# W_dec in one transfer, the gathers in four steps, the last chunks split singly, and a new order of five engines

## What is computed

```python
# block 1: a linear layer whose matrix is decoded per sequence, then a mixture of 8 experts, 2 per token
U = (mu @ W_dec + b_dec).reshape(B, 129, 30)          # mu: 128 x 64, W_dec: 64 x 3870
param = einsum('bik,kj->bij', U, V)                   # weight = first 128 rows, bias = last row
c = einsum('bsd,bde->bse', x, weight) + bias
gate = c @ Wg.T + bg; scores, idx = top_k(gate, 2); w = softmax(scores)
h = gelu(einsum('td,ehd->teh', c, W1) + b1)           # 8 experts, 256 hidden
x = x + sum over the two chosen of w * (h @ W2 + b2)
# block 2: conditioning, then a gated feed-forward with 512 hidden
h = LN(LN(x; tables by pathway); tables by compartment); t, s: LN(x; tables); m, n, r: x + small MLPs
cat = [w0*h, w1*t, w2*m, w3*n, w4*r, w5*s]            # w = softmax(aw)
y = LN(silu(cat @ int_W1 + int_b1) @ int_W2 + int_b2)
f = silu(y@w1.T*s1) * (y@w2.T*s2); f = gelu(f@h1.T*g1); f = gelu(f@h2.T*g2)
x = x + f @ w3.T * s3
```

## Time and profile before

| | |
|---|---|
| median of three runs | 443.49 us (441.01 to 443.49) |
| profiled execution | 443.04 us, span 441.2 us |
| PE, busy share of the span | 94% |
| DVE | 72% |
| ACT | 66% |
| POOL | 32% |
| mean granted TensorE clock | 0.978 |

### The profile page before, as it was taken

How to read it: one execution, slowest core, us unless ns; L and a number is a source line. 1 busy time by engine, 2 the same in 40 slices (tenths; PEclk the granted TensorE clock), 3 DMA queues, 4 the chain that set the end, 5 groups by cost and what they waited for, 6 DMA issues and landing times.

```text
span 441.2 us, 5719 instructions
## 1 busy us (share of the span) xinstructions
PE 416.0 (94%) x1804; PEld 272.6 (62%) x1804; DVE 315.6 (72%) x651; ACT 290.7 (66%) x515; POOL 142.8 (32%) x129
## 2 busy tenths in 40 slices
PE   4888998999999999999999999999999997999994
PEld 2856544554656765677567665776577646687773
DVE  2889998887985776766886577596784687656542
ACT  1568775797937766497647763975678455776563
POOL 3016896663631650273028261317211012010000
PEclk9799996999999999999999999999999998999999
DMA  8975564473352352532315245035501100000000
GB/s 242 364 293 161 179 174 119 112 229 68 104 155 51 71 163 97 118 99 73 111 40 159 75 116 150 0 70 181 134 3 49 46 3 0 1 0 25 0 25 27
DMA packets 29961, 45.08 MB, mean 102 GB/s; under 512 B 3461, under 2 KB 22378, under 8 KB 29418
## 3 DMA queue, kind: packets, MB, share of 16 engines
q1 hardware_dynamic: 25440, 32.33, 25.7%
q0 software_dynamic: 3584, 10.49, 7.1%
...
## 4 chain that ended last, share of the span: by engine, by line
PE 79%; DVE 8%; ACT 5%; issue 3%; DMA 2%; POOL 2%; another core or an unknown queue 1%; ACTq 0%; POOLq 0%; DVEq 0%
PE bank L644 23%; PE bank L746 20%; PE bank L692 7%; PE bank L636 6%; PE bank L782 6%; PE bank L731 5%; PE bank L823 2%; PE bank L660 2%; DMA muT<-cond_512T_in 2%; PE bank L699 2%; PE bank L771 2%; POOL rstd L1446 1%; ACT mG L890 1%; ACT YN L895 1%
## 5 line engine op out<-in xcount | busy, mean ns | idle before, releaser
L644 PE MATMUL bank<-mG,W 128*128 128x512 f32 x256 | 121.3, 604 | 0.1
L890 ACT ACTIVATE mG<-bank,keepP 128x512 f32<-128x512 f32 x128 | 85.3, 685 | 32.2 <-PE bank L636 30.2
L1446 POOL TENSOR_TENSOR rstd<-ve,mhalf 128x4 f32<-128x4 f32 x24 | 34.0, 1419 | 173.0 <-DVE ve L1196 172.1
L1181 DVE TENSOR_TENSOR mG<-mG,gwbs 128x1024 f32<-128x1024 f32 x64 | 77.1, 1220 | 8.8 <-ACT mG L890 4.4
L644 PEld LDWEIGHTS bank<-mG,W 128*128 128x128 f32 x256 | 48.4, 194 | 44.2 <-issue 39.9
L636 PE MATMUL bank<-ts,A 96*128 96x512 f32 x128 | 66.8, 553 | 1.3 <-ACT mG L890 1.1
L955 ACT ACTIVATE G<-bank,keepP 128x512 f32<-128x512 f32 x48 | 32.8, 696 | 25.4 <-PE bank L746 20.1
L1427 POOL DMA_INDIRECT gp<-pgb_in,ixall x32 | 36.8, 1149 | 27.4 <-DVE norms L1233 17.7
L1430 POOL DMA_INDIRECT gcm<-ctm,ixcm x32 | 36.5, 1140 | 9.8 <-issue 9.8
L746 PE MATMUL bank<-hA_h,h1w_h 128*128 128x512 f32 x96 | 38.9, 405 | 0.0
L746 PE MATMUL bank<-hA_l,h1w_h 128*128 128x512 f32 x96 | 38.6, 402 | 0.0
...
## 6 DMA issues: line engine op xcount, KB each, us to landing
...
```

Source lines behind the costliest of these rows:

```text
L644: mm = pe.matmul(OACC[:, :], W2[:, e * HC + c, :], mG[n % NMG][:, c, :], start=False, stop=(e == E - 1 and c == HC - 1))
L890: act.activation(mG[e % NMG][:, c % HC, :], HM[n % 2][:, :], ACT.Gelu, bias=b1c[:, c:c + 1]).then_inc(m_gelu, 1)
L1181: dve.tensor_tensor(mine, mine, gate.unsqueeze(1).broadcast_to([P, HC, TT, P]), ALU.mult).then_inc(m_q, 1)
L1446: step(pool.tensor_tensor(rstd[:, n, :], ve[:, n, :], mhalf[:, :], ALU.pow))
```

## The change

1. `Wd` comes by one transfer of 128 partitions on SP's queue, with the first half of the columns on the partitions 0 to 63. The last 30 columns go to a place of their own, `wd_u`. The two zero blocks of `Wp` change sides.
2. ACT's queue begins with `muT` (twice), `wd_u` and b_dec; V, `keepP`, `earlyP` and `bdec_u` follow in their old order.
3. The eighth piece of the turning moves from DVE to ACT.
4. The copies of `keepP` that DVE made between the turning and `Uall` (`sq_`, `hs1`, `cs12`) stand behind `Uall`, ahead of the words.
5. `tab` issues two of a tile's 8 indirect DMAs; there are four words `tab0` to `tab3` for a tile.
6. In the tail of tile 7 the last two chunks of layer 2's output are made singly: two high parts and two low parts of 512 columns in place of one of 1024 each.
7. The words of all five engines stand in a new order. (A `tcl` for DVE is defined, and no word calls it.)

```diff
-        Wd = sb("Wd", [P, KR * (DH + 1)], stack=early)
+        Wd = sb("Wd", [P, KR * DH], stack=early)
...
+        wd_u = gap[0:MU, KA + KR:KA + 2 * KR]
...
-        PIECES = ("v", "v", "v", "a", "v", "a", "v", "v")
+        PIECES = ("v", "v", "v", "a", "v", "a", "v", "a")
...
+        def alone(j, k):
+
+            return j is TAIL["p"] and k >= 3 * FC - 2
+
         def tail_lo(eng, j, k):
 
-            eng.wait_ge(p_lo[j.s], j.n * (FC + 4) + (k + 1 if k < FC else FC + (k - FC) // 2 + 1))
+            eng.wait_ge(p_lo[j.s], k + 1 if k < FC else FC + (k - FC) // 2 + 1 + (alone(j, k) and k % 2))
...
             "POOL": (
-                (0, "tcl0 tcl1 tcl2 srt ix tcl3 tab tcl4 tcl5 rt0 tcl6 tcl7 rt1"),
...
+                (0, "ix tcl0 tab0 tab1 tcl1 tcl2 srt tcl3 tab2 tcl4 tab3 tcl5 rt0 tcl6 tcl7 rt1"),
...
-            load(Wd[0:MU, :], A["W_dec"][:, KR * DH:KR * (D + 1)], ld_wd)
+            load(Wd[:, :], A["W_dec"][:, 0:KR * D].rearrange("m (h c) -> h m c", h=2), ld_wd)
...
-                act.wait_ge(p_g[j.s], j.n * 2 * FC + k - FC + 2)
+                w = 1 if alone(j, k) else 2
+                act.wait_ge(p_g[j.s], k - FC + w)
                 dst = hB if k < 2 * FC else hC
-                act.activation(dst[0][:, c:c + 2, j.cols], j.G[:, c:c + 2, j.cols], ACT.Copy).then_inc(p_hi[j.s], 1)
+                act.activation(dst[0][:, c:c + w, j.cols], j.G[:, c:c + w, j.cols], ACT.Copy).then_inc(p_hi[j.s], 1)
...
-            load(Wd[MU:P, 0:KR * DH], A["W_dec"][:, 0:KR * DH], ld_wd)
             for at in (0, MU):
                 load(muT[at:at + MU, :], A["cond_512T"], ld_wd)
+            load(wd_u, A["W_dec"][:, KR * D:KR * (D + 1)], ld_wd)
+            load(bdec, A["b_dec"][:, 0:KR * D].rearrange("o (i k) -> (o i) k", k=KR), ld_bd)
             load(Vk[:, :], A["V"], ld_v)
             load(keepP[:, :], A["keepP"], ld_v)
-            load(bdec, A["b_dec"][:, 0:KR * D].rearrange("o (i k) -> (o i) k", k=KR), ld_bd)
             load(earlyP[:, :], A["earlyP"], ld_small)
...
-            def tables(b):
+            def tables(b, t):
...
-                for t in range(TT):
-                    j = b * TT + t
...
+                j = b * TT + t
```

More of the change, by code:

```diff
@@ L119, in build @@
         DH = D // 2
-        Wd = sb("Wd", [P, KR * (DH + 1)], stack=early)
+        Wd = sb("Wd", [P, KR * DH], stack=early)
         W1T = sb("W1T", [P, E * H], stack=early)
-        gap = sb("gap", [P, 6656 - KR * (DH + 1) - E * H], stack=early)
+        gap = sb("gap", [P, 6656 - KR * DH - E * H], stack=early)
         VT3 = gap[:, 0:KA]
         bdec = gap[:, KA:KA + KR]
-        bdec_u = gap[0:KR, KA + KR:KA + KR + 1]
+        wd_u = gap[0:MU, KA + KR:KA + 2 * KR]
+        bdec_u = gap[0:KR, KA + 2 * KR:KA + 2 * KR + 1]
         earlyP = sb("earlyP", [P, 10 * P + 3 * NI + E + 3], stack=early)
@@ L164, in build @@
         Wp = hs[:, 0:KR * D].rearrange("m (k i) -> m k i", k=KR)
-        wd = [Wd[0:MU, :].rearrange("m (i k) -> m k i", k=KR), Wd[MU:P, 0:KR * DH].rearrange("m (i k) -> m k i", k=KR)]
-        wd_u = Wd[0:MU, KR * DH:KR * (DH + 1)]
-        turned_wd = [Wp[0:MU, :, DH:D], Wp[MU:P, :, 0:DH]]
+        halves = (slice(0, MU), slice(0, DH)), (slice(MU, P), slice(DH, D))
+        wd = [Wd[rows, :].rearrange("m (i k) -> m k i", k=KR) for rows, _ in halves]
+        turned_wd = [Wp[rows, :, cols] for rows, cols in halves]
         warmA = sb("warmA", [2, P], stack=early)
@@ L300, in weights_done @@
         def weights_done(eng, *ns):
-            eng.wait_ge(w_lo, max((3, 1, 2, 4)[n] for n in ns))
+            eng.wait_ge(w_lo, max((3, 2, 4, 1)[n] for n in ns))
         def wide(v, n):
@@ L308, in build @@
             "PE": (
[17 rows of a table removed]
[16 rows of a table added]
             ),
             "ACT": (
[19 rows of a table removed]
[20 rows of a table added]
             ),
             "DVE": (
[15 rows of a table removed]
[16 rows of a table added]
             ),
             "POOL": (
-                (0, "tcl0 tcl1 tcl2 srt ix tcl3 tab tcl4 tcl5 rt0 tcl6 tcl7 rt1"),
-                (1, "tab rt0 -rt2 rt1"),
-                (2, "tab rt0 -rt2 rt1"),
-                (3, "tab -rt2 rt0"),
-                (4, "tab -rt1 rt0 -rt2"),
-                (5, "tab -rt1"),
-                (6, "tab =rt2 -rt0 -rt1"),
-                (7, "tab -rt0 -rt1 =rt2 -rt2 rt0 rt1 rt2"),
[8 rows of a table added]
             ),
             "SP": (
[5 rows of a table removed]
-                (5, "gb0 ^stored -li gb1 -lx gb2 +lr gb3 +lt"),
-                (6, "gb0 ^stored -li gb1 -lx gb2 gb3 +lt li ~stored"),
-                (7, "gb0 -lx gb1 lr gb2 li gb3 ~stored lx =stored -sor sop"),
[8 rows of a table added]
             ),
@@ L1075, in _ @@
             act.wait_ge(ld_wd, 64)
-            act.wait_ge(wp_zero, 1)
+            act.wait_ge(wp_zero, 2)
             for q in range(8):
@@ L1079, in _ @@
                     mine = slice(4 * q, min(4 * q + 4, KR))
-                    act.activation(turned_wd[1][:, mine, :], wd[1][:, mine, :], ACT.Copy)
-                    act.activation(turned_wd[0][:, mine, :], wd[0][:, mine, 0:DH], ACT.Copy).then_inc(wd_act, 1)
+                    act.activation(turned_wd[0][:, mine, :], wd[0][:, mine, :], ACT.Copy)
+                    act.activation(turned_wd[1][:, mine, :], wd[1][:, mine, :], ACT.Copy).then_inc(wd_act, 1)
             load(w12s[:, :], A["w12T"], ld_w[0])
@@ L1098, in wl @@
                 src, dst = staged[n], split[n]
-                dve.wait_ge(w_hi, (2, 1, 3, 4)[n])
+                dve.wait_ge(w_hi, (3, 2, 4, 1)[n])
                 dve.tensor_tensor(flat(dst[1]), src, flat(dst[0]).bitcast(F32), ALU.subtract).then_inc(w_lo, 1)
@@ L1288, in fl_tail @@
                 else:
-                    dst, w = (hB if k < 2 * FC else hC), 2
-                    dve.wait_ge(p_hi[j.s], j.n * (FC + 4) + FC + (k - FC) // 2 + 1)
+                    dst, w = (hB if k < 2 * FC else hC), 1 if alone(j, k) else 2
+                    dve.wait_ge(p_hi[j.s], FC + (k - FC) // 2 + 1 + (alone(j, k) and k % 2))
                 dve.tensor_tensor(dst[1][:, c:c + w, j.cols], j.G[:, c:c + w, j.cols], dst[0][:, c:c + w, j.cols].bitcast(F32),
@@ L1358, in s_m, with tcl @@
                 dve.tensor_scalar(awx[:, 1:2], awx[:, 0:1], -1.0, None, ALU.mult).then_inc(aw_max, 1)
+            def tcl(b):
+                dve.wait_ge(tc_hi, b + 1)
+                dve.wait_ge(ts_stored[b % 2], 16 * ((b - 1) // 2))
+                dve.wait_ge(tc_lo, b)
+                dve.tensor_tensor(tsS[b % 2][32:64, :], tT[b % 2][:, :], tsS[b % 2][0:32, :].bitcast(F32), ALU.subtract).then_inc(tc_lo, 1)
             steps = {"q": q_, "x": x1_, "st": st, "t": t_, "s": s_, "hg": hg, "hc": hc, "oh": oh, "a": a, "flo": flo,
@@ L1363, in _ @@
                      "for": partial(fo_tail, TAIL["r"]), "fop": partial(fo_tail, TAIL["p"]), "al": lambda i, n: al(n), "am": lambda i: s_m(),
-                     "wl": lambda i, n: wl(n), "lm": lambda i: low_sum(), "la": lambda i: low_any(),
+                     "wl": lambda i, n: wl(n), "lm": lambda i: low_sum(), "tcl": lambda i, b: tcl(b), "la": lambda i: low_any(),
                      "tb": lambda i, b: tb(b), "gxl": lambda i, g: gxl(g), "bl": lambda i: b2l(), "gl": lambda i: g96l(), "top": lambda i, g: top(g), "gww": lambda i, g: gww(g),
@@ L1378, in _ @@
             dve.wait_ge(ld_wd, 64)
-            dve.wait_ge(wp_zero, 1)
+            dve.wait_ge(wp_zero, 2)
             for q in range(8):
@@ L1382, in _ @@
                     mine = slice(4 * q, min(4 * q + 4, KR))
-                    dve.tensor_copy(turned_wd[1][:, mine, :], wd[1][:, mine, :])
-                    dve.tensor_copy(turned_wd[0][:, mine, :], wd[0][:, mine, 0:DH]).then_inc(wd_dve, 1)
-            sq_()
-            step(dve.tensor_scalar(hs1[:, :], fsc[:, 0:FC], 0.5, None, ALU.mult))
-            dve.tensor_tensor(cs12[:, :], hs1[:, :], fsc[:, FC:2 * FC], ALU.mult)
+                    dve.tensor_copy(turned_wd[0][:, mine, :], wd[0][:, mine, :])
+                    dve.tensor_copy(turned_wd[1][:, mine, :], wd[1][:, mine, :]).then_inc(wd_dve, 1)
             for q in range(0, 8, 2):
@@ L1403, in _ @@
             ins.then_inc(g8_ready, 1)
+            sq_()
+            step(dve.tensor_scalar(hs1[:, :], fsc[:, 0:FC], 0.5, None, ALU.mult))
+            dve.tensor_tensor(cs12[:, :], hs1[:, :], fsc[:, FC:2 * FC], ALU.mult)
             run(steps, ORDER["DVE"])
@@ L1424, in tables @@
                     weights_done(pool, 3)
-                for t in range(TT):
-                    j = b * TT + t
-                    pool.indirect_dma_start(out=gp[b % 2][:, t, :], out_offset=None, in_=A["pgb"],
-                                            in_offset=bass.IndirectOffsetOnAxis(ap=ixall[:, 0, j:j + 1].bitcast(U32), axis=0))\
-                        .then_inc(gat[b % 2], 16)
-                    pool.indirect_dma_start(out=gcm[b % 2][:, t, :], out_offset=None, in_=CT,
```

(14 more changed lines are left out.)

## The result

The changed kernel takes 468.13 us (median of 4 runs, 466.69 to 469.13), the kernel before 443.49 us beside it. The ratio is 1.0565, with a 95% interval of 1.0516 to 1.0614: it is slower by 5.6%, where the prediction said 434.0 us. The profiled execution took 466.69 us, with a span of 464.7 us and a mean clock of 0.955.

What follows compares the result with a forecast made beforehand. PE was taken as full from 120 to 360 us, so gains lie where it idles or is slowly clocked: 443.04 - 4.5 (start) - 3.5 (tiles 0 and 1) - 1.1 (end) = 434.0 us, range 429.5 to 441.0.

Steps and rivals of the forecast that it cites:

- I take 7.0: Beginning: all of Wd lands at 7.0 us, between 6.3 at the earliest and 7.5, so copying starts 4.1 us sooner.
- Start: Beginning up to tm0: first product at 8.0 us, tm0 at about 17.6; 4.5 us saved, from 1.1 to 5.3.
- Rival B: Beginning: bdec_u still lands at 16.6 us, so the start gives only 1.1 us; 437.3 us in all, chance 0.14.
- Tiles 0 and 1: 46 to 120 us: a slow GpSimd subtraction no longer stops PE at the gate scores; 3.5 us saved, upper bound 5.8.
- rival A: Before 115 us: the saving in tiles 0 and 1 goes to other waits of PE; 437.4 us, chance 0.20.
- 2.0 us: Tiles 0 and 1: DVE's own idle time, the sure part of the saving there.
- Rival D: Tile 0: POOL's root late behind a slow tcl5, so the kernel is slower; 447.0 us, 450.4 with late start; chance 0.07.
- Middle: 120 to 360 us: gathers and roots stay ahead of their readers, PE busy 239 us or more of 240; nothing gained or lost.
- the rest: Everything behind the beginning: 3.5 us saved in tiles 0 and 1, 1.1 at the end, all else at nothing.
- End: Tail of tile 7: single last chunks save 1.1 us (0.6 to 1.4); PE's last wait 1.4 us or less, from 2.21.
- the 1.9 us: Beginning: cost of the first four microseconds of products at clock 0.53, expected to vanish with idle time of about 1.3 us.

Runs made afterwards that it cites:

- b_start: Kernel before with the changed beginning, Wd in two 64-partition transfers, single last chunks, wd_u on its own semaphore, bdec_u ahead of V: 437.91 us, ratio 0.9900.
- b_two: Changed kernel with the old words, gathers and paired last chunks put back, and Wd in two transfers of 64 partitions on SP's queue: 441.41 us, ratio 0.9968.
- a_two: Changed kernel with Wd loaded by two transfers of 64 partitions on SP's queue in place of one of 128: 447.97 us, ratio 1.0108.
- b_gm: Kernel of b_start with only PE's gate scores gm4 and gm5 of tile 1 moved behind B and O1: 437.20 us, ratio 0.9872.
- a_lt: Kernel of a_two with only SP's words changed: tile 6's ts load later, one gate load behind the store: 442.43 us, ratio 1.0000.

## Why the prediction was wrong

**The step that failed** is the first of the sum: "0.99 MB [...] at the 259 GB/s of 2 to 8 us", "I take 7.0". It took the rate of all engines for a transfer that only two of them carried. `Wd` landed at 28 us, the first product started at 29.94 in place of 8.0: 21.9 us, two thirds of the 32.7 us between the forecast and the profiled execution. For a transfer on all engines the estimate was 1.1 us short: two transfers on the same queue had landed at 8.12 us in `b_start` (1.38 + 6.74), and the first product followed 0.97 us later, as forecast. The trace of before couldn't show that two engines would carry it, since its two halves had 64 rows each; the access pattern in the diff could. The Trainium skill, "DMA: Bandwidth & Descriptors", section "Why a DMA increments its semaphore by 16 and not by 1", says how many engines share a transfer: the largest number up to 16 that divides the slowest dimension of both access patterns. For 2 x 64 rows against 128 partitions that is 2, and the counts of 2.0, 3.9, 8.1 and 14 to 15 packets agree with it. The section of the Trainium skill that the prediction weighed, "Issuing engines are not separate DMA queues" of the same page, says that all transfers run on the same 16 engines and interleave, and nothing of how many of them one transfer gets.

**Start, apart from the shape.** With two transfers `Wd` was there at about 8.2 us, not at 7.0, and the copying waited for `wd_u` until 9.6 us: I had counted it among "small transfers" and given it no time. The first product came at 10.5 and the products began at a low clock, so that `b_two` gained some 1.5 us of the 4.5. `b_start` mends both, with its first product at 9.09 and full clock; with it the kernel is 4.4 us under the one before (ratio 0.9900, the single chunks included), about what was forecast for the start. Rival B (the second gate) was not the cause: in `a_two` VectorE waited 1.3 us for the last part of b_dec, and the products still ended last.

**Tiles 0 and 1: the waits went as forecast, the gain in time isn't shown.** The gate scores cost PE 0.7 us in place of 2.4, and the clock is 1.00 from 82 to 96. The slow subtraction is still there:

```profile
80.59 7.10 POOL L1454 TENSOR_TENSOR tsS<-tT,tsS 32x512 fp32r<-32x512 f32 x1 [9.71 <-ACT tsS L856]
```

and nobody waits for it. Idle time and clock gave 2.1 + 3.4 = 5.5 us. Of these the next 42 us took back 1.0 us idle and 0.04 x 42 = 1.7 us by the clock, which leaves 2.8, against 3.5 forecast: half of the relief was lost again behind it, so rival A came true in part. `b_gm`, which moves the gate scores alone, is 2.1 us ahead at 108 us, near the "2.0 us" that the prediction called sure, and 0.7 by the medians. Rival D did not happen.

**Middle: the reading that failed second**, a term that was put at nothing. "From 120 to 360 I find every gather and root ahead of its reader": I followed GpSimd and PE there, and not SP. The text itself gave the number that would show the mistake, PE busy for 239 us of 240 or more, and from 138 to 378 it was 235.52. It is rival A in kind (another wait takes the place), 4.8 us by `a_lt`, but A looked for it before 115 us, and it stands near 220 us in `a_two`, near 235 in the changed kernel. The start (4.5 forecast as saved, 17.9 lost) and the rest (4.6 forecast as saved, 5.6 lost) make up the 32.7 us but for rounding: 22.4 + 10.2.

**End: right in the trace** (last wait 0.8 us, bound 1.4; the last products are followed by the result at 460.80), and not measurable in time.

**Clock.** After 22.8 us idle the first four microseconds of products ran at 0.54, as before the change after 5.3 us (0.53), so the 1.9 us that the forecast took as saved were not. In the window with the wait for keep 3.4 us idle came with 1.6 us by the clock, half as much again.
